# A grouped convolution inside a fused attention and feed-forward kernel: position stretches streamed past 64-column weights in place of per-position weights

## The reference

```python
x = x + attn(cond(x, cond_128))       # cond: per sequence a 32x32 mix of rows, plus a shift
                                      # attn: 32 heads of 16, causal over the 32 rows, Wo, bo
x = x + ffn(cond2(x, cond_128))       # cond2: the convolution below; ffn: silu(x w1) * (x w3), w2,
                                      # each weight with a low-rank part of rank 16
# cond2
out = lax.conv_general_dilated(x, weight, window_strides=(1,), padding=[(4, 4)],
                               dimension_numbers=('NCH', 'OIH', 'NCH'), feature_group_count=4)
out = out + ctx[:, :, None] + bias[None, :, None]    # ctx: one number per sequence and channel
```

## Time and profile before

| | |
|---|---|
| median of three runs | 621.25 us (620.95 to 621.43) |
| the profiled execution | 623.67 us |
| its span, first to last instruction | 621.9 us |
| mean granted TensorE clock | 0.992 |
| busy: PE, PEld, DVE, ACT, POOL | 610.1, 501.5, 227.6, 173.7, 174.6 us |
| DMA | 55.10 MB in 36671 packets |

### The profile page before, as it was taken

The page is one execution under the profiler, slowest core; times in us unless marked ns, Lnnn a source line. Parts: engine busy times, 40 slices in busy tenths (PEclk is TensorE's granted clock), DMA queues, the critical chain, the costliest instruction groups (busy, mean ns, idle before and its releaser), DMA issues.

```text
span 621.9 us, 8095 instructions
## 1 busy us (share of the span) xinstructions
PE 610.1 (98%) x3303; PEld 501.5 (81%) x3303; DVE 227.6 (37%) x324; ACT 173.7 (28%) x295; POOL 174.6 (28%) x128
## 2 busy tenths in 40 slices
PE   9999999799999999999999999999999999999997
PEld 6988987677777788888888888798888889888885
DVE  1434553989995451111242111133111115111112
ACT  3561323566552453233111111121111111111110
POOL 3447525779998464444000000000000000000000
PEclk9999999789999999999999999999999999999999
DMA  7965655835846440000016000006100001200001
GB/s 233 357 272 198 208 194 168 250 93 158 195 142 207 164 85 0 1 1 0 1 70 134 1 0 1 1 1 175 28 0 0 0 0 51 85 0 1 0 1 67
DMA packets 36671, 55.10 MB, mean 89 GB/s; under 512 B 11392, under 2 KB 19968, under 8 KB 35392
## 3 DMA queue, kind: packets, MB, share of 16 engines
q1 hardware_dynamic: 35776, 53.29, 28.0%
q10 hardware_dynamic: 864, 1.38, 0.6%
HBM read 36.82 MB, written 16.79 MB: 86 GB/s over the span
## 4 chain that ended last, share of the span: by engine, by line
PE 84%; DVE 8%; POOL 3%; ACT 2%; DMA 1%; issue 1%; SPq 0%; DVEq 0%; ACTq 0%
PE twin L1242 39%; PE twin L1263 19%; PE twin L1084 7%; PE twin L1138 6%; POOL probs L590 3%; DVE total L919 3%; PE twin L1209 3%; PE twin L1104 2%; PE twin L1117 2%; DVE top L902 2%; ACT probs L753 2%; PE twin L1047 1%; PE twin L1195 1%; PE twin L1073 1%; DVE probs L911 1%
## 5 line engine op out<-in xcount | busy, mean ns | idle before, releaser
L988 DVE TENSOR_TENSOR gate<-twin,gate 128x512 f32<-128x512 f32 (+1 forms) x44 | 30.4, 691 | 255.5 <-PE twin L1242 255.5
L1242 PE MATMUL twin<-c_hi,f_hi 128*128 128x512 f32 (+1 forms) x352 | 96.0, 394 | 0.6 <-DVE c_lo L959 0.6
L1242 PE MATMUL twin<-c_hi,f_lo 128*128 128x512 f32 (+1 forms) x352 | 96.4, 395 | 0.0
L1242 PE MATMUL twin<-c_lo,f_hi 128*128 128x512 f32 (+1 forms) x352 | 95.7, 393 | 0.0
L1242 PEld LDWEIGHTS twin<-c_hi,f_lo 128*128 128x128 f32 (+1 forms) x352 | 65.7, 187 | 16.5
L1242 PEld LDWEIGHTS twin<-c_hi,f_hi 128*128 128x128 f32 (+1 forms) x352 | 65.2, 185 | 17.0 <-issue 1.0
L1242 PEld LDWEIGHTS twin<-c_lo,f_hi 128*128 128x128 f32 (+1 forms) x352 | 65.3, 185 | 16.1
L798 ACT ACTIVATE gate<-twin 128x512 f32<-128x512 f32 (+1 forms) x44 | 26.4, 600 | 165.9 <-PE twin L1242 165.9
L1263 PE MATMUL twin<-f_lo,gate_hi 128*128 128x512 f32 (+1 forms) x176 | 69.5, 395 | 0.0
L801 ACT CAST gate_hi<-gate 128x512 fp32r<-128x512 f32 (+1 forms) x44 | 27.3, 620 | 128.2 <-DVE gate L988 128.2
L1263 PE MATMUL twin<-f_hi_head,gate_hi 128*128 128x512 f32 x128 | 50.7, 396 | 0.0
(11 more groups left out here) (141 smaller groups left out, 813.7 us busy)
## 6 DMA issues: line engine op xcount, KB each, us to landing
f_sb<-in_f SPq DMA_DIRECT2D x2, 2752.0 KB, 19.8
x_dram<-resid_stage SPq DMA_DIRECT2D x16, 256.0 KB, 2.0
rows<-x_dram SPq DMA_DIRECT2D x16, 256.0 KB, 3.2
q_t<-q_dram SPq DMA_DIRECT2D x8, 512.0 KB, 4.3
x_dram<-rows SPq DMA_DIRECT2D x16, 256.0 KB, 2.8
near<-x_dram SPq DMA_DIRECT2D x16, 256.0 KB, 7.1
rows<-x_dram SPq DMA_DIRECT2D x4, 1024.0 KB, 6.0
out<-rows SPq DMA_DIRECT2D x16, 256.0 KB, 2.1
```

What stands on the lines that cost most here:

```text
L988: dve.tensor_tensor(gate[0:w, h % 2, :], up_bank[2 * (h % 2) + 1][0:w, :], gate[0:w, h % 2, :], ALU.mult).then_inc(gate_ready, 1)
L1242: mm = pe.matmul(bank[0:w, :], f[:, c, :], c_part[:, c, :], start=(n == 0 and c == 0), stop=(n == 2 and c == DC - 1))
```

## The change

x1 is kept in DRAM as [2, 2048, 256]: the odd and the even half of the positions, each as four stretches of 64 (position 8w + 2r + h is element w of stretch r in half h). For that, Wo's columns, the residual and bo are permuted by POOL and ScalarE at strides of 2 and 8, the rows of f1 and f3 (four loads of 32 partitions each) and the low-rank factors follow, and the last addition writes the outputs back in the old order into `out_slot`.

`near` becomes [128, 16, 64] for each of four channel groups; its partitions are 4 parts of 32 = (8 channels, 4 stretches): the odd half shifted by one, the even half, the odd half, the even half shifted by one. A group is loaded with four DMAs of 512 pieces of 252 or 256 B. The stationary operand is now the group's weights, `conv_sb[:, g]`, 64 columns (2 halves x 4 stretches x 8 channels); 512 columns of `near` stream past it, once for each half of the 32 stretch windows, to output partitions 0 to 63 and 64 to 127: 8 float32 matmuls of 512 columns for a block. VectorE transposes each 128x512 result from PSUM in 32x32 blocks (`turn_conv`), and adds the shift in SBUF. TensorE builds `conv_sb` out of the old weights with 26 small matmuls at n = 2 of the attention loop (`group_conv`), ScalarE copies it.

The groups of blocks 1 to 3 move to steps 8 and 9 of the block before, two behind each up step; those of block 0 stand together at n = 16. near for block 0 is issued at n = 11 and n = 13. f1 is taken before f3 in a step, and the first step of a block waits for c_hi first and for c_lo one third later. The shift is loaded for one block at a time.

```diff
-            for r in range(BT):
-                    sp.dma_start(near[r * S:(r + 1) * S, :, 1:P + 1],
-                                 x1_near[r, :, bass.ds(i * BB, BB), :]).then_inc(near_loaded, 16)
+        near_parts = ((1, slice(1, WIN), slice(0, WIN - 1)), (0, slice(0, WIN), slice(0, WIN)),
+                      (1, slice(0, WIN), slice(0, WIN)), (0, slice(0, WIN - 1), slice(1, WIN)))
+            def load_near(i, g):
+                for a, (half, to, of) in enumerate(near_parts):
+                    sp.dma_start(near[g][a * S:(a + 1) * S, :, to],
+                                 x1_near[half, g * S:(g + 1) * S, bass.ds(i * BB, BB), of])\
+                        .then_inc(near_loaded[g // 2], 16)
...
-            pool.memset(near[:, :, 0:1], 0.0).then_inc(near_zeroed, 1)
-            pool.memset(near[:, :, P + 1:P + 2], 0.0).then_inc(near_zeroed, 1)
+            pool.wait_ge(wo_lo_split, REP)
+            for pair in (near_head, near_tail):
+                pool.memset(pair[:, :, :, 0:1], 0.0).then_inc(near_zeroed, 1)
+                pool.memset(pair[:, :, :, WIN - 1:WIN], 0.0).then_inc(near_zeroed, 1)
...
+            def turn_conv(i, g, bank):
+
+                dve.wait_ge(conv_filled, i * GROUPS + g + 1)
+                dve.transpose(c_raw[:, g, :, :, :].rearrange("p b r o -> p (b r o)"), bank[:, :]).then_inc(c_turned, 1)
+
+            def add_conv_shift(i, g):
+
+                dve.wait_ge(c_turned, i * GROUPS + g + 1)
+                shift = convb_block[:, :].rearrange("p (b s) -> p b s", s=S)[:, :, g * CG:(g + 1) * CG]
+                dve.tensor_tensor(c_raw[:, g, :, :, :], c_raw[:, g, :, :, :],
+                                  shift.unsqueeze(2).to_broadcast([P, BB, BT, CG]), ALU.add).then_inc(c_ready, 1)
...
-                for b in range(BT):
-                    for m in range(NEAR):
-                        mm = pe.matmul(bank[:, b * P:(b + 1) * P], near[:, q * BT + b, m:m + P],
-                                       conv_sb[:, m, :], start=(m == 0), stop=(m == NEAR - 1))
+            def group_conv():
+
+                pe.wait_ge(conv_loaded, 16)
+                pe.wait_ge(conv_zeroed, 1)
+                to = ps[7][:, 0:GROUPS * 2 * S].rearrange("p (g h q o) -> p g h q o", g=GROUPS, h=2, q=BT)
+                for a, high in ((0, 1), (BT - 1, 0)):
+                    pe.matmul(to[a * S:(a + 1) * S, :, high, :, :].rearrange("p g q o -> p g (q o)"), ident_sb[:, 0:S],
+                              conv_sb[:, :, 0, :, :].rearrange("p g q o -> p g (q o)"), start=True, stop=True)
+                for g in range(GROUPS):
+                    own = slice(g * CG, (g + 1) * CG)
+                    for a in range(BT):
+                        for high in range(2):
+                            if 0 <= a - high < NEAR:
+                                mm = pe.matmul(to[a * S:(a + 1) * S, g, high, :, :], ident_sb[:, g * S:(g + 1) * S],
+                                               conv_raw[:, a - high, :].rearrange("k (q o) -> k q o", o=S)[:, :, own],
+                                               start=True, stop=True)
+                mm.then_inc(conv_grouped, 1)
+
+            def convolve(i, g, bank):
+
+                if g % 2 == 0:
+                    pe.wait_ge(near_loaded[g // 2], 16 * 2 * len(near_parts) * (i + 1))
+                for half, part in enumerate(rows_of):
+                    mm = pe.matmul(bank[part, :], conv_sb[:, g, :, :, :].rearrange("k h r o -> k (h r o)"),
+                                   near[g][:, :, half * S:(half + 1) * S], start=True, stop=True)
                 mm.then_inc(conv_filled, 1)
...
-                if more:
-
-                    convolve_block(i + 1)
-                down(i, HC - 2, first)
+                for h in range(1, HC):
+                    up(i, h, first, more)
+                    if more and h in (CONV_AT, CONV_AT + 1):
+
+                        pe.wait_ge(gate_ready, i * HC + h)
+                        for g in (2 * (h - CONV_AT), 2 * (h - CONV_AT) + 1):
+                            convolve(i + 1, g, up_bank[(g + 2) % 4])
+                    down(i, h - 1, first)
                 down(i, HC - 1, first)
```

More of the change, by code:

```diff
@@ L161, in adaln_attention_ffn @@
         near_zeroed = sem("near_zeroed")
-        near_loaded = sem("near_loaded")
+        near_loaded = [sem(f"near_pair{n}_loaded") for n in range(2)]
         x1_loaded = sem("x1_loaded")
@@ L210, in adaln_attention_ffn @@
             y_hi = sb("y_hi", [P, DC, BLOCK], room, F32R)
-        convb_all = sb("convb_all", [P, N])
+        with ExitStack() as room:
+            convb_block = sb("convb_block", [P, BLOCK], room)
+            gate = sb("gate", [P, 2, BLOCK], room)
+            out_spare = sb("out_spare", [P, D], room)
+        sb("room9", [P, N])
         with ExitStack() as room:
@@ L236, in adaln_attention_ffn @@
             f2_hi_head = sb("f2_hi_head", [P, F2_HEAD, D], room, F32R)
-            near = sb("near", [P, BB, P + 2], room)
-        sb("room3", [P, F2_HEAD * D + BB * (P + 2)])
+            near_head = sb("near_head", [P, 2, BB, WIN], room)
+        with ExitStack() as room:
+            sb("room3_head", [P, F2_HEAD * D], room)
+            a_up_s = sb("a_up_s", [STACK, 2, D], room, F32R)
+        sb("room3", [P, F2_HEAD * D + 2 * BB * WIN])
         with ExitStack() as room:
@@ L504, in load_rows @@
             def load_rows(i):
-                sp.dma_start(rows[:, :, :], x1_rows[:, bass.ds(i * TILES, TILES), :]).then_inc(x1_loaded, 16)
+                for h in range(2):
+                    sp.dma_start(rows[:, :, h * D // 2:(h + 1) * D // 2],
+                                 x1_rows[:, bass.ds(i * TILES, TILES), h, :]).then_inc(x1_loaded, 16)
             def store_out(i):
@@ L989, in block_of_rows @@
                                       ALU.mult).then_inc(gate_ready, 1)
+                    pair = (2 * (h - CONV_AT), 2 * (h - CONV_AT) + 1) if more and h in (CONV_AT, CONV_AT + 1) else ()
+                    for g in pair:
+                        turn_conv(i + 1, g, up_bank[(g + 2) % 4])
                     dve.wait_ge(gate_hi_ready, i * HC + h + 1)
@@ L1225, in up @@
-            def up(i, h, first):
+                    for g in range(GROUPS):
+                        convolve(0, g, first_conv_bank[g])
+            def up(i, h, first, more):
                 w, cols = HW[h], slice(h * P, h * P + HW[h])
-                if first:
-                    pe.wait_ge(lo_split, parts_split(h, 1))
-                    if h == 1:
-                        pe.wait_ge(down_folded, 6)
+                if first and h == 1:
+                    pe.wait_ge(down_folded, 6)
                 if h >= 2:
@@ L1234, in up @@
                     pe.wait_ge(gate_ready, i * HC + h - 1)
-                for parts, bank, filled in (
-                        (((f1_hi[:, :, cols], c_hi), (f1_hi[:, :, cols], c_lo), (f1_lo[:, :, cols], c_hi)),
+                if more and h in (CONV_AT + 1, CONV_AT + 2):
+                    pe.wait_ge(c_turned, (i + 1) * GROUPS + 2 * (h - CONV_AT))
+                for which, parts, bank, filled in (
+                        (1, ((f1_hi[:, :, cols], c_hi), (f1_hi[:, :, cols], c_lo), (f1_lo[:, :, cols], c_hi)),
@@ L1268, in block_of_rows @@
             def block_of_rows(i, first, more):
-                pe.wait_ge(c_lo_ready, BT * (i + 1))
-                up(i, 0, first)
+                pe.wait_ge(c_hi_ready, GROUPS * (i + 1))
+                up(i, 0, first, more)
                 if first:
```

228 lines of the change are left out of this document (123 added, 105 removed).

## The result

The changed kernel takes 604.17 us (median of 4 runs, 601.42 to 605.45) against 621.25 us before: ratio 0.971, 95% interval 0.969 to 0.974. The forecast of 597.7 us was 6.5 us too low, inside its range of 591.5 to 608. The profiled execution took 603.86 us with a span of 602.1 us, so the same 1.8 us lie around it as before.

The account below looks back on a forecast made before the run. TensorE was taken as the bound, with 84% of the chain, alone from 190 us on. Terms -19.3 (three blocks), -6.2 (block 0), +1.2, +0.5 and +0.2 give -23.6: 621.25 to 597.7 us, range 591.5 to 608.

Parts of the forecast that it names:

- Part 1: Convolution as 512-column matmuls on TensorE: 6.4 us less in each of blocks 1 to 3, 6.8 less in block 0.
- The doubted step: Convolution records writing the two output halves run side by side; rival without overlap: 608.5 us, within a case given 0.15.
- Part 2: Waits around the convolution in a block: new VectorE work fits with 1 us cover, costed at nothing; end +0.2 us.
- Part 3: Start of attention: regrouping the convolution's weights +1.1 us, with wo_lo and memsets together +1.2 us.
- The dip of the clock: TensorE's lower granted clock from 118 us in attention, kept unchanged: zero, bounds -2.8 and +2 us.
- Part 4: DMA queue: near hidden in blocks 1 to 3; for block 0 the queue is full, scores 14 late by +0.5 us.
- The line through 2 KB and 512 B: Near's DMA price from the 84 ns and 43 ns rows: 38 ns per 256 B piece, 19.6 us a block.
- the second rival: Cheap DMA queue (22 ns a piece) and the attention clock dip goes: 592.9 us, chance 0.10.
- The rival with dear pieces: Near's 256 B pieces are dear and scores 14 wait: 621.7 us, with f2 late 623 to 626, chance 0.07.
- Part 5: Entry into the first block: between -7.7 and -5.1 us with tile 15 late, taken as -6.2.
- the two delays of attention: The +1.2 us at attention's start and the +0.5 us of scores 14 waiting for q and k loads.
- the sign that the prediction named itself: Forecast wrong if TensorE waits over 3 us for near_loaded or k_wide, or POOL's additions wait for their rows.

Follow-up runs that it names:

- r5: r2 with both halves of each group in blocks 1 to 3 written to the lower 64 output rows: 604.54 us.
- r9: r2 with only the lower half convolved in blocks 1 to 3: 598.01 us.
- r2: The changed kernel with f1 and f3 each loaded in one transfer, their rows reordered beforehand: 596.1 us, ratio 0.960.
- r4: The kernel before with f1 and f3 each in four loads of 32 neighbouring partitions, source and order unchanged: 630.36 us, ratio 1.014.
- r6: r2 with block 0's near loads issued by ScalarE, one group of four per step, instead of SyncE: 591.7 us, ratio 0.952.
- r3: r2 with the four matmuls of a pair of groups ordered lower, lower, upper, upper instead of alternately: 595.5 us, ratio 0.960.
- r12: The best version with 512 and 128 B left free, so tiles lie where they did in the kernel before: 594.62 us, ratio 0.957.
- r8: The kernel before with one 512 B constant allocated last, so all tiles behind it lie 512 B lower: 621.73 us, ratio 1.001.
- r11: The kernel before with three small constants allocated last, so all tiles behind them lie 768 B lower: 621.3 us, ratio 1.000.
- r1: The changed kernel run again with nothing altered: 601.47 us, ratio 0.970.

## Why the prediction came out as it did

**Part 1, the convolution on TensorE: right, in size and in cause.** The doubted step was the overlap of the two halves, read off the product with v; r5 and r9 show it for the new form. The time of one record was taken at 0.43 and is 0.43 from start to start, 0.45 to 0.47 with the ends. The slots were one too many: a pair takes four record times (1.87 us), not five (2.15). Against that the down step behind each pair takes 2.96 us instead of 2.72. Together a block saves 10.72 - 2 x 1.87 - 2 x 0.24 = 6.5 us; 6.4 was forecast. Block 0 saves 7.2 (10.7 - 3.5), forecast 6.8.

**Part 2, the waits in the blocks: right.** TensorE waits at no block boundary.

**Part 3, the start of attention: too dear, by a row of another form.** The regrouping was taken at 3.3 us, at least 0.064 us for each of 52 records. It took 0.8 (119.69 to 120.50):
```profile
119.69 0.30 PE L1198 MATMUL twin<-conv_sb,ident_sb 128*32 128x128 f32 x2
...
119.84 0.73 PE L1205 MATMUL twin<-conv_raw,ident_sb 128*32 128x32 f32 x41
120.50 0.51 PE L1241 MATMUL twin<-mask,mask_rows 64*128 64x512 f32 x2
```
The nearest rows had 128 columns of data; 48 of these 52 records have 32, and 32-column weights to four parts of the output rows. Which of the two makes them cheap no run separates. wo_lo's stride of 2 costs nothing to speak of (5.10 against 5.01 us), where a stride-4 row had been the upper bound. In r2, which has no delay in front of it, the first subtraction starts at 106.21, 0.5 us before that of the kernel before, and the third block's mixing is already 0.5 us ahead (61.89 against 62.38 us): this term is about zero, not +1.2. The dip of the clock was kept in the forecast, and it stayed: the granted clock is 0.54 from 130 to 133 us, behind a wait of 3.04 us, and the projection there takes 4.52 us.

**The loads of f1 and f3: missing.** This is the step that failed. The diff has them, one transfer each turned into four of 32 partitions, and the prediction gives them no term. They cost 6.9 us of the profiled run up to attention, and more behind it; r2 gains 5.4 us at the median by undoing them, and 11.2 us between the two profiled spans. The trace of before held the warning: near's loads, also of 32 partitions each, moved at half the rate of the whole rows. The prediction put that down to the size of the pieces alone. r4 has pieces of the old size and halves the rate all the same.

**Part 4, the queue: right in the outcome, wrong in the price and in the cause.** Pieces of 256 B were taken at 38 ns. With near alone in the queue the changed kernel shows (328 to 330 us)
```profile
328.00:330.00 2.00, 2.00 (x11) 1.65 (x9) 1.16 (x2) 0.62 (x1) 0.00 (x0) 1.00 1.31 234
```
234 GB/s: one piece in 1.1 ns, 17.5 ns for each of 16 engines, and each of near's loads landed 2.6 to 4.7 us behind its issue. The line through 2 KB and 512 B was drawn through two things at once, the piece and the number of partitions. (It also gives 36 ns and not 38 by its own two points, which moves nothing.) So of the second rival the cheap queue is what happened and the end of the clock's dip is not, and scores 14 waited for nothing. The rival with dear pieces falls. The Trainium skill (DMA: Bandwidth & Descriptors, Specifications) has transfers under 512 B do read-modify-write; no run here shows a cost of it: 256 B pieces move at 234 GB/s where 512 B pieces moved at 190, though the two forms differ in more than the piece. The prediction also said that no transfer from DRAM in pieces under 512 B stands in the trace of before; the load of the causal mask, in pieces of 128 B, does, though it is too small to give a rate. What near did cost was never in the sum: 16 issues of 0.6 to 0.7 us on SyncE, 11 us where four had taken 2.2, in the middle of the chain of stores and loads of one tile after the other. f2 was forecast at 199.4 because the data were late; in r2 it goes out at 196.57 because the issues were, and r6, where the same data are issued by another engine, issues f2 3.9 us earlier and has a median 4.4 us lower.

**Part 5, into the first block: too cautious without the loads, and overrun with them.** Up step 1 was worked out as 216.5, and the sum put it at 219.7 (224.2 - 6.2 + 1.2 + 0.5). In r2 it comes at 216.06, 3.7 us before that: neither of the two delays of attention arose, and the late tile 15 cost less than was set aside. In the changed kernel it comes at 227.2, 11.1 later: 7.4 are there when up step 0 starts (214.32 against 206.94), 2.1 are the longer wait for f_lo (4.19 against 2.07), and the rest is the low clock behind it. The prediction had the cause of that wait (tile 15's rows behind f2: 11.45 us from issue to landing, where it took 10.6), but not its size, nor what a TensorE that has stood idle pays afterwards. By the sign that the prediction named itself, additions on GpSimd that wait for their rows, its account of the queue fails here: the last addition waits 4.96 us for tile 15's rows (2.82 in r2).

**The pace.** Some 3.5 us of gain (23.1 in the blocks, less 3 x 6.5 for the convolution) that no reading of the instructions could give.

The sum, then, forecast against the profile: the front 0 against +6.9 (the loads); attention, queue and transition together -4.5 against -4.0, where r2 without the loads' wait has -7.7; the blocks -19.3 against -23.1 (6.5 each, and the pace); the tail +0.2 against +0.4. In all -23.6 against -19.8. The missing term and the gain of the pace have opposite signs and hide each other in part. That the result lies inside the range is in part luck.

The best version, r7, takes 591.1 us: the change with f1 and f3 in one load each, near issued by ScalarE in block 0, and tile 15 ahead of f2. It is 4.9% faster than the kernel before, where the change alone is 2.9%.

## What to carry to other kernels

Go through a diff by its transfers before its arithmetic, and give each one whose shape changes a term, even where it was far from the chain: a load that had 9 us to spare and is cut into quarters by partition is on the chain. Count the issues on the queue that runs a store-and-load chain, not only their bytes; here moving 16 issues to another engine lowered the median by 4.4 us, although the two profiled executions are equally long. And read a rate off a row only if it has the same number of partitions and the same piece, one at a time.

## What the runs showed of the hardware

- Two matmuls with 64-column weights that write different halves of the output rows run at the same time: 8 records in 1.87 us, 4 of one half alone in 1.86, 8 to the same half in 3.58. They need not be neighbours: with four records of one half ahead of four of the other the eight also take 1.87 us (r3).
- Eight loads into 32 partitions each moved 200 to 213 GB/s where two into 128 partitions moved 418 to 429, at the same share of the engines and with the same source (r4). Number of loads and partitions of each were not changed separately.
- Pieces of 256 B moved at 234 GB/s, more than pieces of 512 B into rows of 520 B at 190.
- In a row of eight, issuing one load took SyncE 0.6 to 0.7 us, of 256 B pieces as of a k_wide head (5.86 and 5.14 us against 5.10 for eight).
- Moving tiles by 512 B in front of near and by 640 B behind it changed TensorE's pace by 1.2% (8.37 against 8.27 us per step, r12 against r7); moving all of them together by 512 or 768 B did not (r8, r11).
- In the first block, idle stretches of TensorE of 2.06 (r3), 2.33, 2.61, 2.64 (r1), 4.19 and 4.47 us were followed by matmuls at the low clock, one of 2.07 us (r2) was not; in attention one of 1.94 us and one of 2.26 (r6) were, one of 1.38 (r2) was not. The length alone does not tell them apart.
